# Two attentions in a one-core network: late splits and value tiles behind the first eight maxima, exponential's table loaded early

## What is computed

```
def _L3_attn_ref(x, Wq, Wk, Wv, Wo, bo):
    B, S, D, H = (4, 512, 256, 16)
    HD = D // H
    b, s, d = x.shape
    q = (x @ Wq).reshape(b, s, H, HD).transpose(0, 2, 1, 3)
    k = (x @ Wk).reshape(b, s, H, HD).transpose(0, 2, 1, 3)
    v = (x @ Wv).reshape(b, s, H, HD).transpose(0, 2, 1, 3)
    scores = jnp.einsum('bhqd,bhkd->bhqk', q, k)
    causal = jnp.tril(jnp.ones((s, s), dtype=bool))
    scores = jnp.where(causal, scores, -jnp.inf)
    attn = jax.nn.softmax(scores / np.sqrt(HD), axis=-1)
    ctx = jnp.einsum('bhqk,bhkd->bhqd', attn, v)
    ctx = ctx.transpose(0, 2, 1, 3).reshape(b, s, d)
    return ctx @ Wo + bo
...
t = t + _L2_attn_ref(_ln_t(t), L2_attn_w_qkv, L2_attn_w_proj, L2_attn_b_proj)
t = t + _L2_ffn_ref(_ln_t(t), L2_ffn_gate_w, L2_ffn_w1, L2_ffn_w2, L2_ffn_w3)
t = t + _L3_attn_ref(_ln_t(t), L3_attn_Wq, L3_attn_Wk, L3_attn_Wv, L3_attn_Wo, L3_attn_bo)
t = t + _L3_ffn_ref(_ln_t(t), L3_ffn_Wg, L3_ffn_W1, L3_ffn_W2, L3_ffn_W3)
```

## The kernel before

SP issues the twelve loads of each of the first four stacks, then waits and goes on:

```
            sp.wait_ge(s_lo, SPLITS)

            for g in range(GROUPS - 1):

                sp.wait_ge(s_s2, UNITS * g + 1)
                prefetch(sp, g)
                if g >= 1 and g + 3 < GROUPS:

                    load_stacks(g + 3)
```

## Time and profile before

| | us |
|---|---|
| median of 3 runs | 1021.78 (1020.67 to 1025.45) |
| profiled execution, its own time | 1023.44 |
| its span | 1021.7 |
| TensorE busy | 825.4 |
| VectorE busy | 451.4 |
| ScalarE busy | 301.5 |
| layer 2's attention, about | 269 to 378 |
| layer 3's attention, about | 578 to 690 |

### The profile page before, as it was taken

One profiled execution on the slowest core, in us unless ns is written; L12 is line 12 of the kernel. 1 busy time (PEld: TensorE's weight loads), 2 busy tenths in 40 slices (PEclk: granted clock), 3 DMA queues, 4 the chain that ended last, 5 costly groups with the idle time before them and its releaser, 6 DMA issues. The chain is left out here.

```text
span 1021.7 us, 12512 instructions
## 1 busy us (share of the span) xinstructions
PE 825.4 (81%) x3900; PEld 519.2 (51%) x3901; DVE 451.4 (44%) x1165; ACT 301.5 (30%) x478; POOL 233.2 (23%) x314
## 2 busy tenths in 40 slices
PE   3769378899687885399999187876399999999993
PEld 2758236434444544266666144544156666565652
DVE  4974531698766644522222556644521212121213
ACT  3223135532245561122212144452022222212121
POOL 1140000473201000334433113340211221122110
PEclk8569677999799995699999697896599999999996
DMA  3000070000136502042111436832003016601004
GB/s 109 1 0 1 1 257 0 1 1 0 48 96 188 152 2 91 19 124 83 46 46 37 145 82 191 246 104 91 15 16 145 22 30 267 267 21 31 21 18 132
DMA packets 53618, 80.36 MB, mean 79 GB/s; under 512 B 10020, under 2 KB 45988, under 8 KB 50372
## 3 DMA queue, kind: packets, MB, share of 16 engines
q1 hardware_dynamic: 48040, 67.37, 20.5%
q0 software_dynamic: 5536, 12.46, 4.1%
HBM read 55.82 MB, written 11.27 MB: 66 GB/s over the span
## 5 line engine op out<-in xcount | busy, mean ns | idle before, releaser
L2083 PE MATMUL psum<-ring,f_x_t 128*128 x552 | 252.1, 600 | 1.3 <-DVE f_x_t L1951 1.3
L1944 DVE TENSOR_TENSOR f_gated<-f_silu,psum 128x512 f32<-128x512 f32 x69 | 47.5, 688 | 268.8 <-PE psum L2083 268.8
L2083 PEld LDWEIGHTS psum<-ring,f_x_t 128*128 128x128 f32 x552 | 101.0, 193 | 103.2 <-issue 103.1
L2097 PE MATMUL psum<-ring,f_gated_t 128*128 x552 | 130.7, 380 | 1.8 <-ACT f_gated_t L2010 1.8
L2097 PEld LDWEIGHTS psum<-ring,f_gated_t 128*128 128x128 f32 x552 | 101.4, 190 | 23.3 <-issue 12.7
L2010 ACT ACTIVATE f_gated_t<-psum 128x512 f32<-128x512 f32 x69 | 41.2, 597 | 235.3 <-PE psum L2090 235.3
L2006 ACT ACTIVATE f_silu<-psum 128x512 f32<-128x512 f32 x69 | 41.2, 597 | 113.3 <-PE psum L2083 113.3
L1529 PE MATMUL psum<-a_stack_k,a_stack_q 96*128 96x256 bf16 (+1 forms) x256 | 43.5, 276 | 15.9 <-DVE a_maxima L1341 5.9
L1815 POOL DMA_INDIRECT f_xs<-rows_in,f_from_now x48 | 47.5, 989 | 36.5 <-POOL f_from_now L1812 36.5
L1812 POOL COPY f_from_now<-f_from_row 128x1 uint32 (+1 forms) x48 | 9.0, 187 | 204.7 <-PE psum L2076 201.1
L1824 POOL DMA_INDIRECT rows_out<-f_y,f_to_now x46 | 46.0, 1001 | 36.4 <-POOL f_to_now L1821 35.3
(11 more groups left out here) (293 smaller groups left out, 1229.0 us busy)
## 6 DMA issues: line engine op xcount, KB each, us to landing
ring<-in_f_experts SPq DMA_DIRECT2D x24, 1536.0 KB, 7.8
a_stack_q<-a_parts SPq DMA_DIRECT2D x96, 64.0 KB, 2.1
a_stack_k<-a_parts SPq DMA_DIRECT2D x96, 64.0 KB, 2.0
rows_in<-h SPq DMA_DIRECT2D x4, 1024.0 KB, 5.8
ring<-rows_out SPq DMA_DIRECT2D x8, 512.0 KB, 5.4
a_wqkv<-in_a_wqkv SPq DMA_DIRECT2D x2, 768.0 KB, 4.4
x_in<-in_x SPq DMA_DIRECT2D x1, 1024.0 KB, 5.2
out<-x SPq DMA_DIRECT2D x4, 256.0 KB, 2.1
```

The costliest lines, as they stand in the source:

```text
L1944: dve.tensor_tensor(gated[:, b, :], silu[:, b, :], psum[:, 2 * b + 1, :], ALU.mult).then_inc(s_g, 1)
L2083: last = pe.matmul(psum[:, 2 * b + side, :], x_t[:, xb, t, :], k.ring[:, bass.ds(at + start, CHUNK)], start=(t == 0), stop=(t == CT - 1))
L2097: last = pe.matmul(psum[:, Y_BANK, 0:C], gated_t[:, b, P * a:P * a + P], k.ring[:, bass.ds(at + start, C)], start=(c == 0 and a == 0), sto ...
```

## The change

Pieces 5 and 6 move behind the eighth and ninth maximum, piece 7 into the loop (projected in unit 0, into bank 7). Value tiles 4 and 5 are projected behind the second and fifth maximum, tiles 6 and 7 in units 2 and 3. On ScalarE an exponential of one column, whose result nobody reads, stands right behind the square roots, so that its table is loaded there. The waits are set accordingly: the loop starts when 7 remainders and 2 value copies are done, and `weigh_values` waits for the value copies it needs.

```diff
-VALUES_AFTER = (GROUP - 2, GROUP - 1, GROUP, GROUP + 2)
+VALUES_AFTER = (1, 4)
...
-SPLITS_AFTER = (0, 2, 4)
+SPLITS_AFTER = (GROUP - 1, GROUP)
...
-    return i if i < SPLITS // 2 else 2 + i % 2
+    return i if i < SPLITS // 2 else 7 if i == SPLITS - 1 else 2 + i % 2
...
             for i in range(FIRST_MAXIMA):
                 take_max(i)
-                if i in SPLITS_AFTER:
-                    take_rest(SPLITS_BEFORE + SPLITS_AFTER.index(i))
-                if i - 1 in SPLITS_AFTER:
-                    take_low(SPLITS_BEFORE + SPLITS_AFTER.index(i - 1))
                 if i == GROUP - 1:
                     negate(0)
+                if i - 1 in SPLITS_AFTER:
+                    take_rest(SPLITS_BEFORE + SPLITS_AFTER.index(i - 1))
+                    take_low(SPLITS_BEFORE + SPLITS_AFTER.index(i - 1))
...
                     for ahead in maxima_ahead(i):
                         take_max(ahead)
+                    if i == 0:
+                        take_rest(SPLITS - 1)
+                    if i == 1:
+                        take_low(SPLITS - 1)
...
             ln.deviation(act)
+            act.activation(inverse[:, 0, 0, 0:1], ln.sd[:, 0:1], ACT.Exp)
...
-            for i in range(SPLITS // 2, SPLITS):
+            for i in range(SPLITS // 2, SPLITS_BEFORE):
                 split(i)
+            take_values(2)
...
             negate(0)
-            for i in range(TT // 4, TT // 2):
-                take_values(i)
+            for i in range(SPLITS_BEFORE, SPLITS - 1):
+                split(i)
...
                                    ACT.Exp, scale=HD ** -0.5).then_inc(s_ex, 1)
+                    if i == 0:
+                        take_high(SPLITS - 1)
+                    if i == 1:
+                        take_middle(SPLITS - 1)
+                    if i == 3:
+                        take_values(TT // 2 - 1)
...
                 pe.wait_ge(s_sel, 2 * quad + 2)
+                if quad == 0:
+                    pe.wait_ge(s_vo, TT // 2 - 1)
+                if quad == QUADS:
+                    pe.wait_ge(s_vo, TT // 2)
...
-            pe.wait_ge(s_r, SPLITS)
+            pe.wait_ge(s_r, SPLITS - 1)
             pe.wait_ge(s_ones, 1)
             pe.wait_ge(s_ones_rows, 16)
-            pe.wait_ge(s_vo, TT // 2)
+            pe.wait_ge(s_vo, 2)
...
                         weigh_values(i // 2 - 1)
+                    if i == 0:
+                        project_part(SPLITS - 1)
+                    if i == 2:
+                        pe.wait_ge(s_r, SPLITS)
+                        project_values(TT - 2)
+                    if i == 3:
+                        project_values(TT - 1)
```

More of the change, by code:

```diff
@@ L1405, in split, with take_high, take_middle @@
             def split(i):
+                take_high(i)
+                take_middle(i)
+            def take_high(i):
                 act.wait_ge(s_qk, i + 1)
                 act.activation(part_of(i, 0), psum[:, split_bank(i), :], ACT.Copy).then_inc(s_hi, 1)
+            def take_middle(i):
                 act.wait_ge(s_r, i + 1)
@@ L1479, in project_part @@
                 column = C * which + P * t_out
-                if i >= 4:
+                if i >= SPLITS // 2:
                     pe.wait_ge(s_r, i - 1)
```

## The result

| | before | after |
|---|---|---|
| median of 20 runs each | 1022.61 us | 1026.36 us |
| lowest and highest | 1020.67, 1027.94 | 1021.18, 1030.17 |
| span of the profiled execution | 1021.7 us | 1027.5 us |
| its own time | 1023.44 us | 1029.16 us |
| its mean granted clock | 0.875 | 0.878 |

The ratio is 1.0033, with a 95% interval of 1.0019 to 1.0047: the changed kernel is 3.75 us slower by the medians (3.4 by the ratio). The mean clock of the profiled execution was not lower, so a generally slower clock is not the cause.

The account below looks back on a forecast made before the run. The prediction took the landing of group 1's row of maxima, which releases the loop's fifth pair, as the bound. Layer 2's +3.7 and layer 3's +2.2 made +5.9 us on 1021.78: 1027.7 us, range 1021.5 to 1032.0.

Parts of the forecast that it names:

- the likeliest case: The forecast's own case, with the fifth pair released by the row's landing: 1026 to 1029.5 us, chance 0.45.
- the sum: Total over both attentions: 3.7 us in layer 2 plus 2.2 in layer 3, +5.9 us.
- Term 1: Layer norm's end: early table load delays the copy before the first projection, +1.5 us per attention on everything behind.
- Rival D: ScalarE empties itself at the early load, between last square root and copy: 1030.3 us, chance 0.05.
- Term 2: Loop's start: the table load ahead of the first exponential goes; it gains 0.46 us, the total 0.
- Term 3: Reordered maxima and splits: without the early load, 18th maximum 0.4 us earlier in layer 2, 0.7 later in layer 3.
- Term 4: SP's wait for low parts puts the ring load 1.0 us before group 1's row; layer 2's fifth pair +3.7 us.
- Layer 3, +2.2: Layer 3's fifth pair: landing stays behind a ring load, so 0.7 + 1.5 = +2.2 us.
- rival C: TensorE's slow clock moves onto split projections and values in units 2 and 3: +2 to +5 us, chance 0.2.
- Step 5: Last value tiles in units 2 and 3: 1.9 us of TensorE covered by the landing, 0; otherwise the next bound.
- Rival A: The first pair decides the fifth, so the earlier loop carries through: 1017.3 to 1020.3 us, chance 0.1.
- B, short landing: Group 1's row slips past the ring load in 2.9 us, so the moved values decide: 1026.2 us, chance 0.2.

Follow-up runs that it names:

- e2: Kernel before with only the early exponential (table load) added behind the layer norm's last square root: 1025.85 us, ratio 1.0033.
- e10: Kernel before with the early table load placed behind the copies of the first two turned columns: 1023.65 us, ratio 1.0001.
- e5: Changed kernel with its early exponential moved behind the first two copies of turned tokens: 1024.66 us, ratio 1.0023.
- e7: Changed kernel with only the first ring load issued earlier, ahead of the fourth stack's loads: 1023.54 us, ratio 1.0010.
- e8: Kernel before with only the first ring load issued earlier, ahead of the fourth stack's loads: 1029.87 us, ratio 1.0063.
- e4: Changed kernel with the first ring load ahead of the fourth stack's loads, later ones between a stack's query and key loads: 1038.38 us, ratio 1.0148.
- e11: Changed kernel with SyncE's wait for the low parts moved from the first ring load to the ring's own stacks' first loads: 1028.41 us, ratio 1.0052.
- e9: Changed kernel with the early exponential behind the first two copies and the first ring load ahead of the fourth stack's loads: 1022.64 us, ratio 1.0005.
- e3: Changed kernel with value tiles 6 and 7 projected and copied ahead of the loop again: 1028.69 us, ratio 1.0061.
- e6: Changed kernel without the early exponential and with value tiles 6 and 7 ahead of the loop again: 1026.05 us, ratio 1.0028.
- e1: Changed kernel without the early exponential, all moves of splits and values kept: 1026.45 us, ratio 1.0044.
- e12: e9's kernel with two unread matmuls added behind the scores of each of maxima 3 to 12: median 1029.08 us; ratio 1.0012 from seven runs only.

## Why the prediction was right, point by point

The forecast was 1027.7 us, the median is 1026.36, inside the range and inside the likeliest case's 1026 to 1029.5. Slower by over 0.5% was given 0.57 and within 0.5% 0.39; with 1.0033 it is the latter. The direction and the two mechanisms were right; that the number is so near has luck in it. Against the runs the sum (+5.9, measured +3.75) was 2.2 us too large. The time is only 1.3 too high since its base, 1021.78 from three runs, was 0.8 below the 1022.61 of twenty. And the sum's shares are wrong in both layers. The steps one by one:

- **Term 1, early table load, +1.5 per attention on the path: right at the first projection, not "on everything behind".** First projection +1.6 in both; e2 measures 3.4 us for it alone, against 3.0, and e10 shows that its place alone costs. But the agreement of 3.4 with 3.0 is partly luck: in layer 2 of e2 it is the landing that makes it. In the changed kernel the first maximum of layer 2 was only 0.8 later, and covering the load there gave back 1.4 us (e5), half of the term. Rival D (a pause beside the load) is excluded: 0.02 and 0.01 us on either side. The Trainium skill (ScalarE: Activation LUTs, What ACT_TABLE_LOAD costs) puts a drain of 1.38 us beside each load; neither this kernel nor e10 shows it.
- **Term 2, the load taken from the first exponential, 0: right.** The first exponential started 3.7 us earlier, with the pair, and the fifth pair was later.
- **Term 3, order up to the 18th maximum: the working was 2.1 us too late.** It gave 315.0 + 1.5 = 316.5; the trace has 314.42. The shift of 1.5 had become 0.9 by the first maximum (0.6 of it), the eight maxima took 5.3 instead of 5.7 us (0.3), the ninth came 0.2 sooner behind them, from the ninth maximum to the first pair it was 0.7 less than worked out, and from there to the 18th 0.3. That the 18th maximum does not gain what the first pair gains held in the main: the first pair came 3.3 us earlier, the 18th maximum 1.0.
- **Term 4, the row behind the ring load: the mechanism was right, its cause incomplete, its size 2 us too large in layer 2.** The landing (5.5 said, 5.0 to 5.6 measured) and the wait for it came as said; e7 and e8 show it from two sides, and e4's rows landed in 1.8. But `s_lo` alone doesn't set the ring load: SyncE's own 48 loads, which the prediction left out, end within 0.24 us of it, and e11 without that wait gained nothing. The fifth pair was +1.7, not +3.7, since the row was issued at 316.0 instead of 318.1: term 3's error, passed on. The two prices of the landing, 1.9 to 2.9 and 5.4 to 5.5, are also one thing (see the last section): the row lands about when the ring load does.
- **Layer 3, +2.2: measured +3.3 at the fifth pair and +4.4 at the end.** Not from the landing, but from half clock over the moved values, as rival C has it, worked out there at up to 2 us. Where the clock there was mostly at its upper level (0.84 in the 10.5 us up to the pair), the pair is 1.5 to 1.7 later than before, with the landing long (e5, e11) or short (e7, e9): the prediction's path, through the landing, was not the one that decides in this layer.
- **Step 5, values covered in units 2 and 3, 0: right at full clock, and right that they are the next bound** (e9). e3 suggests that ahead of the loop they would cost more, its interval overlapping the changed kernel's.
- **Rival A, the earlier loop carries: wrong.** The distance from first to fifth pair grew from 9.6 to 14.6 us in layer 2. **B, short landing: no** (in no attention of the changed kernel). The count against it was misread, though: the kernel before has eight rows issued within 2 us behind a ring load, not seven, and the one at 669.4 landed in 4.7. **C, the clock moves: partly**, in layer 3 for the worse and at the end of layer 2 for the better; the execution's mean clock (0.878, before 0.875) was not lower.

That the profiled execution's own difference, +5.7, is so near to +5.9 is partly chance. By the block starts 0.2 of its longer span came ahead of layer 2, -0.4 in it, 1.0 between the attentions, 4.4 in layer 3 and 0.6 behind, so 1.8 lies outside the attention, in code that the change doesn't touch, and the two layers' shares are not those of the forecast (3.7 and 2.2).

**Open.** e6 says that the moved splits alone cost 3.7 us, e2 that the table load alone costs 3.4, and the whole change costs 3.75. That the costs share the landing fits e2, whose fifth pair waits for it, and e7, which gets back 2.6 while it keeps both the splits and the table load. But e1 (both layers) and e6 (layer 2) also show half clock in the first maxima, where e2 and the changed kernel don't, and no run separates the two causes there: e12 was meant to and didn't. Of the 2.6 us of e7's edit the fifth pairs show about 1; where the rest comes from is not traced.

## What to carry to other kernels

A short, urgent DMA that a bulk load of another queue precedes by a microsecond waited here for the bulk load: look for where the issuing engine's own queue lets that load out, and move it to where nothing urgent follows (e7), not just anywhere else (e4, e8). A table load cost 3.4 us on the path and nothing that could be seen two copies further down, beside work that ScalarE had to wait for anyway (e2, e10). A delay also costs by what it moves next to what: 1.5 us brought a ring load closer in front of a row (e2). Bringing the loop's start forward by 3 us was worth nothing, since a later item of the loop is tied to the same serial work as before.

## What the runs showed of the hardware

The landing of the two small DMAs of a row, by how long after a ring load (1.5 MB) they were issued:

| | first issue behind the ring load | landing |
|---|---|---|
| before, layer 2 | 4.7 us | 1.9 to 2.9 us |
| e7, layer 2 and 3 | 9.9 and 9.2 us | 1.6 to 1.9 us |
| e9, layer 2 and 3 | 10.9 and 10.6 us | 1.6 us |
| before, layer 3 | 0.7 us | 5.4 to 5.5 us |
| changed, layer 2 and 3 | 1.0 and 1.2 us | 4.9 to 5.6 us |
| e8, group 0, layer 2 and 3 | 1.8 and 0.7 us | 5.9 to 6.7 us |

The rows leave by GpSimd's queue and the ring loads by SyncE's. Over all 14 profiles (224 rows, both attentions):

| issued behind the last ring load by | rows | landing |
|---|---|---|
| up to 2.3 us | 111 | 3.7 to 7.5 us |
| 4.7 to 6.5 us | 5 | 1.9 to 4.3 us |
| 9 us or more | 83 | 1.6 to 3.6 us |
| no ring load yet, only stack loads | 25 | 1.6 to 2.2 us |

So there are not two prices. The row's landing goes with that of the ring load itself. In the kernel before that takes 7.7 us in layer 2 and 6.6 in layer 3:

```profile
L1655 SPq DMA_DIRECT2D ring<-in_f_experts x1: 521/521/521, 312.3 to 312.3; - x1
DMA to landing us min/median/max: 7.7/7.7/7.7
...
L1655 SPq DMA_DIRECT2D ring<-in_f_experts x1: 526/526/526, 622.6 to 622.6; - x1
DMA to landing us min/median/max: 6.6/6.6/6.6
```

That is 320.0 and 629.2, and the fifth pairs, released by the row, start at 320.44 and 629.33. In all 76 rows issued within 7 us behind a ring load whose landing the profile has, the later of the row's two DMAs landed after the ring load, by 0.1 to 2.4 us, half of them by under 0.5. So the 2.9 us of layer 2 before was the rest of a ring load too. The Trainium skill (DMA: Bandwidth & Descriptors, Queues, rings and completion order) says that a DMA engine takes turns between queues at packet granularity; whatever the turns, a separate queue did not spare the small transfer 3 to 4 us here. The 48 stack loads of 64 KB that run beside the first rows did not hold them up.

Unexpected too: SyncE issued its stack loads at 0.65 us each without a gap for 31 us, so that a queue of 48 small loads held back a bulk load, and taking away the semaphore wait behind them (e11) let it go at most 0.3 us earlier.
